# Routing of a mixture layer inside a joined attention stream: one wide comparison per sequence, sums on GpSimd, its events spread over two sequences, one bias product per sequence's logits

## What is computed

```python
def _L2_ffn_ref(x, router_w, router_bias, ...):          # x: (4, 1024, 128), 32 experts
    logits = flat @ router_w.T + router_bias
    scores = softmax(logits, axis=-1)
    topk_scores, topk_idx = top_k(scores, 4)
    topk_scores = topk_scores / clip(topk_scores.sum(-1, keepdims=True), 1e-12, None)
    ...                                                   # every token: sum over its 4 experts of score * expert(x)
```

## Time and profile before

| | |
|---|---|
| time, median of 3 runs | 2736.76 us (2734.14 to 2738.77) |
| profiled execution, its time | 2752.16 us |
| profiled execution, its span | 2750.4 us |
| PE / DVE / ACT / POOL busy | 82% / 59% / 46% / 27% |
| mean granted PE clock | 0.887 |
| the joined stream | about 660 to 2110 us of the span |

### The profile page before, as it was taken

One profiled execution on the slowest core, in us unless ns is written; L12 is line 12 of the kernel. 1 busy time (PEld: TensorE's weight loads), 2 busy tenths in 40 slices (PEclk: granted clock), 3 DMA queues, 4 the chain that ended last, 5 costly groups with the idle time before them and its releaser, 6 DMA issues. The chain is left out here.

```text
span 2750.4 us, 44402 instructions
## 1 busy us (share of the span) xinstructions
PE 2246.2 (82%) x15454; PEld 1301.6 (47%) x15454; DVE 1633.4 (59%) x3420; ACT 1260.7 (46%) x1914; POOL 752.9 (27%) x886
## 2 busy tenths in 40 slices
PE   3788878884798998999988789999997888776474
PEld 1455555562244444444444334444444775455274
DVE  6767676652674664756747787777772444554202
ACT  2334444332255666656564245565665442332143
POOL 1325253543010110200200132424221114662432
PEclk7878898987798999999999689999999999896687
DMA  2111200004020020111100011222212993110186
GB/s 64 40 48 56 48 9 2 3 1 108 28 74 29 20 61 20 38 43 38 52 28 20 19 44 56 76 61 61 64 51 88 294 314 120 42 42 17 56 275 183
DMA packets 144400, 185.07 MB, mean 67 GB/s; under 512 B 27153, under 2 KB 118450, under 8 KB 139159
## 3 DMA queue, kind: packets, MB, share of 16 engines
q1 hardware_dynamic: 103391, 136.81, 17.0%
q0 software_dynamic: 13696, 32.02, 3.7%
q10 hardware_dynamic: 27126, 13.75, 1.8%
HBM read 129.75 MB, written 52.21 MB: 66 GB/s over the span
## 5 line engine op out<-in xcount | busy, mean ns | idle before, releaser
L1766 DVE TENSOR_REDUCE a_mpart<-a_mx 128x1 f32<-128x512 f32 (+3 forms) x1216 | 744.9, 655 | 297.6 <-PE a_mx L1500 165.2
L1674 ACT ACTIVATE a_prob<-a_st 128x1024 f32<-128x1024 f32 (+3 forms) x768 | 608.1, 812 | 548.8 <-PE a_st L1533 396.4
L1497 PE MATMUL a_mx<-a_ka,a_qa 96*128 96x512 bf16 (+3 forms) x1536 | 438.1, 343 | 71.7 <-DVE a_mpart L1766 38.8
L1530 PE MATMUL a_st<-a_qa,a_ka 96*128 96x512 bf16 (+3 forms) x1536 | 422.5, 337 | 25.8 <-ACT a_prob L1674 14.5
L1548 PE MATMUL a_acc<-a_prob,a_v_aug 128*9 128x512 f32 (+3 forms) x3072 | 329.9, 507 | 0.0
L1497 PEld LDWEIGHTS a_mx<-a_ka,a_qa 96*128 96x128 bf16 x1536 | 142.8, 100 | 359.2 <-DVE a_mpart L1766 180.2
L1533 PE MATMUL a_st<-w_mask_t,identb 128*128 128x128 bf16 x1024 | 211.4, 226 | 0.0
L1530 PEld LDWEIGHTS a_st<-a_qa,a_ka 96*128 96x128 bf16 x1536 | 147.8, 100 | 127.7 <-ACT a_prob L1674 26.0
L1421 POOL DMA_INDIRECT x_rows<-l_xn,l_slots x128 | 124.9, 976 | 267.7 <-ACT a_prob L1674 256.5
L2188 PE MATMUL t_psu<-t_xsT,t_w 128*128 128x128 f32 x960 | 154.2, 296 | 25.9 <-DMA t_w<-in_l_experts 17.3
L1500 PE MATMUL a_mx<-w_mask_q,identb 128*128 128x128 bf16 x768 | 167.5, 227 | 0.0
(11 more groups left out here) (459 smaller groups left out, 4003.9 us busy)
## 6 DMA issues: line engine op xcount, KB each, us to landing
t_w<-in_l_experts SPq DMA_DIRECT2D x160, 192.0 KB, 4.3
t_w<-in_l_experts SPq DMA_DIRECT2D x40, 514.0 KB
a_qa<-q_parts_dram SPq DMA_DIRECT2D x96, 192.0 KB
a_ka<-k_parts_dram SPq DMA_DIRECT2D x96, 192.0 KB
x_rows<-zeros SPq DMA_DIRECT2D x25, 512.0 KB, 3.5
t_xs<-x_rows ACTq DMA_DIRECT2D x40, 256.0 KB, 4.8
y_rows<-t_y POOLq DMA_DIRECT2D x40, 256.0 KB
q_parts_dram<-a_parts SPq DMA_DIRECT2D x24, 256.0 KB
```

Source lines behind the costliest of these rows:

```text
L1497: ins = pe.matmul(to, qa[G % NQ][0:QK_PAD, h0 + k, qi * P:(qi + 1) * P], ka[G % NQ][:, h0 + k, lo:hi], start=not masked_first, stop=k == p ...
L1530: ins = pe.matmul(to[:, lo:HALF], ka[G % NQ][:, h, j * P:(j + 1) * P], qa[G % NQ][0:QK_PAD, h, ch * HALF + lo:(ch + 1) * HALF], start=True ...
L1674: act.activation(prob[:, k_at % NP_, 2 * pair:2 * pair + 2, lo:HALF], sring[s % 2][:, :, lo:HALF], ACT.Exp, scale=1.0 if alibi(G // NG) el ...
L1766: dve.tensor_reduce(mpart[:, G % 2, h0:h0 + per, qi, piece], slot[:, 0:per * width].rearrange("p (k w) -> p k w", k=per), X, ALU.max).then ...
```

## The change

- `r_taken`: DVE makes one comparison for all four choices (128x1024, f32) into `hits`, which lies where `hot` lies later; POOL adds the four planes in two instructions, the second into `taken` in bf16. DVE no longer waits for the result within the event; it waits for it ahead of the next sequence's comparison. `total` on PE waits for four sums rather than for sixteen.
- `r_top` is cut in two halves of four tiles, two positions apart; ranks and shares are an event of their own, `r_shares`.
- `logits`: one product of ones with the bias, repeated for the eight tiles (3x256), opens the bank; the eight tile products add to it.
- Positions, counted from the first of pass 4, a pass being 96: sequences start at 17, 35, 62 and 80; `r_exp` at +2, `r_top` at +4 and +6, `r_shares` at +8, `r_taken` at +10. `total` and `earlier` go to 97 to 107, `r_count` to 103, `r_add` to 109, `r_hot` and `r_slot` to 112 to 130, `r_tiles` to 132, `place` to 134 to 378.
- Row maxima and sums of the softmax lie in `cum` rather than in `rden`.

```diff
-        for b, pos in enumerate((18, 22, 26, 34)):
+        for b, pos in enumerate((17, 35, 62, 80)):
             put_at(at4 + pos, ("logits", b))
-            put_at(at4 + pos + 1, ("r_exp", b))
-            put_at(at4 + pos + 2, ("r_top", b))
-            put_at(at4 + pos + 3, ("r_taken", b))
+            put_at(at4 + pos + 2, ("r_exp", b))
+            for half in range(2):
+                put_at(at4 + pos + 4 + 2 * half, ("r_top", b, half))
+            put_at(at4 + pos + 8, ("r_shares", b))
+            put_at(at4 + pos + 10, ("r_taken", b))
         for half in range(2):
-            put_at(at4 + 42 + 4 * half, ("total", half))
-            put_at(at4 + 50 + 2 * half, ("earlier", half))
-        put_at(at4 + 48, ("r_count",))
-        put_at(at4 + 54, ("r_add",))
+            put_at(at4 + 97 + 4 * half, ("total", half))
+            put_at(at4 + 105 + 2 * half, ("earlier", half))
+        put_at(at4 + 103, ("r_count",))
+        put_at(at4 + 109, ("r_add",))
         for k in range(TOPK):
-            put_at(at4 + 55 + 3 * k, ("r_hot", k))
-            put_at(at4 + 57 + 3 * k, ("r_slot", k))
-        put_at(at4 + 68, ("r_tiles",))
+            put_at(at4 + 112 + 5 * k, ("r_hot", k))
+            put_at(at4 + 115 + 5 * k, ("r_slot", k))
+        put_at(at4 + 132, ("r_tiles",))
         spread([("place", b, k, t) for b in range(BATCH) for k in range(TOPK) for t in range(NT)],
-               at4 + 70, NG * STEPS * (NV - 1) + 90)
+               at4 + 134, NG * STEPS * (NV - 1) + 90)
...
+                        elif kind == "r_taken":                                   # POOL
+                            b = e[1]
+                            pool.wait_ge(hit_s, b + 1)
+                            pool.tensor_tensor(hits[:, 0:2], hits[:, 0:2], hits[:, 2:4], ALU.add).then_inc(pair_s, 1)
+                            pool.wait_ge(pair_s, b + 1)
+                            pool.tensor_tensor(taken[:, :, b * NT:(b + 1) * NT].rearrange("p e t -> p t e"), hits[:, 0], hits[:, 1], ALU.add
+                                               ).then_inc(taken_s, 1)
...
+                            pe.matmul(slot[:, 0:NE].rearrange("p (t e) -> p t e", e=E2), ones3[:],
+                                      B["l2_rbias"].unsqueeze(1).to_broadcast([PARTS, NT, E2]), start=True, stop=False)
                             for t in range(NT):
-                                to = slot[:, t * E2:(t + 1) * E2]
-                                pe.matmul(to, tile_cols(seqs[BATCH + b].xT, t), W["l2_router"][:], start=True, stop=False)
-                                ins = pe.matmul(to, ones3[:], B["l2_rbias"], start=False, stop=True)
+                                ins = pe.matmul(slot[:, t * E2:(t + 1) * E2], tile_cols(seqs[BATCH + b].xT, t), W["l2_router"][:], start=False,
+                                                stop=t == NT - 1)
...
-                            pe.wait_ge(taken_s, TOPK * BATCH)
+                            pe.wait_ge(taken_s, BATCH)
...
                         elif kind == "r_taken":                                   # DVE
                             b = e[1]
-                            if not b:
+                            if b:
+                                dve.wait_ge(taken_s, b)
+                            else:
                                 dve.wait_ge(w2_loaded, 16 * (len(second_loads) + 2))
-                            by_tile = taken[:, :, b * NT:(b + 1) * NT].rearrange("p e t -> p t e")
-                            dve.wait_ge(topped, b + 1)
-                            for k in range(TOPK):
-                                here = bcast(idx[:, k, b * NT:(b + 1) * NT], E2)
-                                if not k:
-                                    dve.tensor_tensor(by_tile, rank_b([P, NT, E2]), here, ALU.is_equal).then_inc(taken_s, 1)
-                                else:
-                                    dve.wait_ge(taken_s, TOPK * b + k)
-                                    link(dve.tensor_tensor(hit, rank_b([P, NT, E2]), here, ALU.is_equal))
-                                    dve.tensor_tensor(by_tile, by_tile, hit, ALU.add).then_inc(taken_s, 1)
-                            dve.wait_ge(taken_s, TOPK * (b + 1))
+                            dve.tensor_tensor(hits, W["rank32"][:].unsqueeze(1).unsqueeze(1).to_broadcast([P, TOPK, NT, E2]),
+                                              bcast(idx[:, :, b * NT:(b + 1) * NT], E2), ALU.is_equal).then_inc(hit_s, 1)
```

More of the change, by code:

```diff
@@ L1283, in attention_layers @@
             NE = NT * E2
-            pr, hit = (w2_flat[:, i * NE:(i + 1) * NE].rearrange("p (t e) -> p t e", e=E2) for i in range(2))
+            pr = w2_flat[:, 0:NE].rearrange("p (t e) -> p t e", e=E2)
             taken = w1[:].bitcast(BF16).rearrange("p (e t) -> p e t", t=N)
@@ L1287, in attention_layers @@
             hot = hT[:, 2:4].rearrange("p c t -> p (c t)").rearrange("p (t e) -> p t e", e=E2)
+            hits = hT[:, 2:4].rearrange("p c t -> p (c t)").rearrange("p (k t e) -> p k t e", k=TOPK, e=E2)
             eight = count[:].rearrange("p k e -> p (k e)")
@@ L1290, in attention_layers @@
                 "p (t k) -> p t k", k=8)
-            r_sum = rden[:].rearrange("p c t h -> p (c t h)")[:, 0:NT]
+            r_max, r_sum = cum[:, 0:NT], cum[:, NT:2 * NT]
             tiles, upto, adjust, ones_e = (count[:, i] for i in range(4))
@@ L1313, in attention_layers @@
             summed = sem(n + "summed")
-            r_exped, topped, taken_s, counted, hot_s, slot_s, slots_set, chosen_s, experts_in = (
-                sem(n + k) for k in ("r_exped", "topped", "taken_s", "counted", "hot_s", "slot_s", "slots_set",
+            r_exped, topped, hit_s, pair_s, taken_s, counted, hot_s, slot_s, slots_set, chosen_s, experts_in = (
+                sem(n + k) for k in ("r_exped", "topped", "hit_s", "pair_s", "taken_s", "counted", "hot_s", "slot_s", "slots_set",
                                      "chosen_s", "experts_in"))
@@ L1857, in _ @@
                             if b:
-                                dve.wait_ge(topped, b)
+                                dve.wait_ge(topped, 2 * b)
                             made_l = slot[:, 0:NE].rearrange("p (t e) -> p t e", e=E2)
-                            link(dve.tensor_reduce(r_sum, made_l, X, ALU.max))
-                            dve.tensor_tensor(pr, made_l, bcast(r_sum, E2), ALU.subtract).then_inc(ring_v, 1)
+                            link(dve.tensor_reduce(r_max, made_l, X, ALU.max))
@@ L1862, in _ @@
+                            dve.tensor_tensor(pr, made_l, bcast(r_max, E2), ALU.subtract).then_inc(ring_v, 1)
                         elif kind == "r_top":
+                            _, b, half = e
+                            if not half:
+                                dve.wait_ge(r_exped, b + 1)
+                                link(dve.tensor_reduce(r_sum, pr, X, ALU.add))
+                                link(dve.reciprocal(r_sum, r_sum))
+                                link(dve.tensor_tensor(pr, pr, bcast(r_sum, E2), ALU.mult))
@@ L1863, in _ @@
+                            for t in range(half * NT // 2, (half + 1) * NT // 2):
+                                ins = dve.max(best8[:, t], pr[:, t])
+                            link(ins)
+                            for t in range(half * NT // 2, (half + 1) * NT // 2):
+                                ins = dve.max_index(at8[:, t], best8[:, t], pr[:, t])
+                            ins.then_inc(topped, 1)
+                        elif kind == "r_shares":
                             b = e[1]
@@ L1864, in _ @@
                             mine = slice(b * NT, (b + 1) * NT)
-                            dve.wait_ge(r_exped, b + 1)
-                            link(dve.tensor_reduce(r_sum, pr, X, ALU.add))
-                            link(dve.reciprocal(r_sum, r_sum))
-                            link(dve.tensor_tensor(pr, pr, bcast(r_sum, E2), ALU.mult))
-                            for t in range(NT):
-                                ins = dve.max(best8[:, t], pr[:, t])
-                            link(ins)
@@ L1872, in _ @@
-                            for t in range(NT):
-                                ins = dve.max_index(at8[:, t], best8[:, t], pr[:, t])
-                            link(ins)
-                            dve.tensor_scalar(idx[:, :, mine].rearrange("p k t -> p t k"), at8[:, :, 0:TOPK], -1.0, float(E2), ALU.mult, ALU.add
-                                              ).then_inc(topped, 1)
+                            dve.wait_ge(topped, 2 * (b + 1))
+                            link(dve.tensor_scalar(idx[:, :, mine].rearrange("p k t -> p t k"), at8[:, :, 0:TOPK], -1.0, float(E2), ALU.mult, ALU.add))
```

## The result

The changed kernel takes 2714.8 us (median of eight runs, 2711.4 to 2726.7); the kernel before, timed beside it, 2738.9 (eight runs, 2734.1 to 2749.4). The ratio is 0.992, with a 95% interval from 0.990 to 0.994. The forecast was 2689, the range ended at 2713: faster it is, by half of what was expected, and 1.8 us outside the range.

A forecast was written before the change was run, and what follows sets the result against it. DVE was taken to bound pass 4. Passes 4 and 5, 371.2 us, would become 293.8 (two plain passes) + 14.7 (PE's work) + 8 (waits) + 7.2 (clock) = 323.7: gain 47.5, forecast 2689 us, range 2674 to 2713.

The forecast's parts named there:

- The comparison, the sums on POOL: Routing: comparison 1.21 us, saving 20.7 us of DVE over four sequences; POOL sums 1.15 and 1.3 us, nothing on the path.
- The bias product: Router logits on PE: 2.9 us per sequence instead of 3.7, so four sequences cost 11.7 us instead of 14.6.
- `r_tiles` on SP now stands beside the load of group 23, whose data are needed 36 steps later: nothing: SP's queue in pass 5: the moved store beside that load was counted as costing nothing.
- pass 5 above 165 us: Sign that the prediction is wrong, with the DVE bound moved to pass 5; forecast for that pass 150 to 160 us.
- The waits, 8 with a bound of 20: PE's waits, passes 4 and 5: 6 us for four sequences, 2 in pass 5's first group; ring covers about 2 us.
- The clock, 0.9 for each us of waiting: PE's clock in passes 4 and 5: each us of waiting brings 0.9 us of clock loss, 7.2 us in all.
- `r_hot`'s 2.86 us on POOL ... Nothing on the path: Pass 5: `r_hot` among the q, k, v pieces, which have ten steps until loaded, was counted as costing nothing.
- The scatters: 128 scatters in 244 positions instead of 308; 16 us cover before DVE's wait for `placed` in pass 6, nothing on the path.
- The spreading, which was to carry the gain: Routing in small pieces over passes 4 and 5 uses DVE's idle time, 34.7 us per pass; waits shrink but not to nothing.
- the bursts still stall PE: Rival 2, passes 4 and 5: waits 12 to 20 us, followed by low clock; gain 25 to 40, 2705 us; chance 0.14.
- Rival 3: POOL's sums lock out DVE in full: 10 us more DVE time, 19 us with the clock, 2708 us; chance 0.05.
- Rival 6: Slower: stalls spread over both passes at clock 0.83, 2747 us; decides once waits and clock loss pass 63 us; chance 0.04.

The follow-up runs named there:

- e4: The changed kernel at its new positions, with the old `r_taken` (comparisons and additions all on DVE) put back: 2732.3 us, ratio 1.000.
- e1: The changed kernel with `r_tiles` at position 133 instead of 132, behind the load of group 23: 2702.3 us, ratio 0.990; timed again, 2701.2 us, 0.988.
- e10: The kernel of e7 timed again: 2696.8 us, ratio 0.985.
- e5: The changed kernel's wide comparison, POOL sums and bias product, with all routing events at their old positions: 2702.7 us, ratio 0.990.
- e6: The changed kernel with the 32 old bias products put back, one behind each tile: 2713.9 us, ratio 0.994.
- e3: The changed kernel with `r_tiles` at 133 and pass 5's q, k, v pieces twelve positions later: 2707.6 us, ratio 0.990.
- e7: The changed kernel with `r_tiles` at 133, the softmax norm as its own event, and what follows two positions later: 2704.7 us, ratio 0.990.

## Why the prediction fell short, step by step

*The bound.* Right. DVE set the end in pass 4: with 22.0 us of its work put back, pass 4 is 20.9 us longer, and passes 4 and 5 together 17.4 (e4).

*The comparison, the sums on POOL.* Right in size: 1.24 us on average for 1.21, POOL 1.27 and 1.32 for 1.15 and 1.3. No wait for `taken` is among PE's.

*The bias product.* Too dear: 2.0 us for a sequence where 2.9 stood. The step took the distance between the two router products and the bias product of the alternating order (0.34 us a tile) as theirs alone; without the alternation a tile takes 0.22. That is 3.7 us in favour of the change (14.7 - 11.0).

*"`r_tiles` on SP now stands beside the load of group 23, whose data are needed 36 steps later: nothing".* This failed, and it cost 11.7 us (e1). It asked when the data would be needed and not what they would stand behind; the queue was named, the semaphore at its head was not. And "36 steps" counted to the group's scores, not to its maxima. It is the largest part of the missing 26 us that one edit takes away. With `r_tiles` moved the time is inside the range (2702.3 and 2701.2), and 14.4 us stay (338.1 in e1 against 323.7), from the waits and the clock below. The prediction had named pass 5 above 165 us as a sign of being wrong and DVE as what would then bound it. The sign came (168.9), and the cause was this load: without it pass 5 is 157.2.

*The waits, 8 with a bound of 20.* Mis-sized: 25.7, or 18.8 without the late load. A piece of 2.2 us was taken to be covered by the ring. It comes behind six operations of the maxima that the ring has to cover too, and then PE stands for 2.33 us. For pass 5's first group 2 us were taken; that group took 50.8 us for 43.1 before, and PE is idle 6.6 us in it where it was 2.0. PE's waits there are 3.6 us for DVE, which had 10.5 us more to do than in pass 6 before (42.34 for 31.81; the prediction said 13), and 2.7 for ACT.

*The clock, 0.9 for each us of waiting.* Mis-sized in kind. After has 25.7 us and 19.3 (0.75), e10 21.6 us (19.4 + 12.3 - 10.1) and 334.7 - 293.6 - 11.0 - 21.6 = 8.5 (0.39). There is no fixed ratio: not every wait brings the lower level.

*"`r_hot`'s 2.86 us on POOL ... Nothing on the path".* Wrong by a few us: ACT waited 10.7 us behind it, and PE for ACT 3.0 us in the rows above.

*The scatters.* Right: no DVE wait for `placed`, and pass 6 unchanged.

*The spreading, which was to carry the gain.* Wrong in weight. It was the centre of the sum, but comparison and bias product bring 28.8 us without it, and it brings 4.3 more even when its SP queue is in order (e5, e1). It is small where the bursts have been made small first. With the old `r_taken` in place the spreading would be worth some 10 us, an estimate: 371.2 before, less e4's 367.0, plus 11.7 for the late load, less 5.6 for the bias product (e6).

Of the rivals, the second comes nearest, "the bursts still stall PE": 12 to 20 us of waits, 2705. With the late load on top it is what happened. Rival 3's mechanism is in the traces, at a fraction of its price. Rival 6, the slower case, is not what was seen: the clock was 0.92 and 0.96, not 0.83, and waits plus clock loss were 45 us, below the 63 from which it decides.

Two things stay open. Whether finer pieces shorten the whole time by 4 us would take more timings; the traces show it for pass 4 alone. And nothing here divides the waits of pass 5's first group between POOL's pieces and DVE's own work, since the edit of e3 moved products of PE and work of DVE along with POOL's pieces.

## What to carry to other kernels

When an event of an order written by hand moves, look on every queue at the waits of what it is put in front of: a DMA that waits for a late result holds each load behind it, though the queue seems empty and the loads need nothing. Put such a store behind the loads of its position. Remove work from the engine that sets the pace before spreading it: in pass 4 each us of DVE work in bursts of 6.6 us cost PE nearly a us even after they were spread (e4), while with no piece above 1.3 us the clock of that pass was 0.94 to 0.98 for 0.92 and 0.93. And when a moved group of events makes one stretch shorter, look at PE's busy time beside its idle time before calling it a gain.

## What was not expected of the hardware

One 128x32 operation of DVE, 0.24 us at its next turn, took 3.11 us in after's pass 5, while POOL had three operations in a row. It ended with the last of them, and took 3.11 and 3.09 us at the same place in e4 and e6:

```profile
1692.91 1.16 POOL L1424 DMA_INDIRECT x_rows<-l_xn,l_slots  x1 [1.28 <-issue]
1693.43 3.11 DVE L1941 TENSOR_SCALAR a_count<-a_count,partition 128x32 f32<-128x32 f32 x1
...
1694.09 1.29 POOL L1447 TENSOR_TENSOR a_f<-a_f,a_hT 128x512 f32<-128x512 f32 x1
...
1695.31 1.18 POOL L1459 TENSOR_TENSOR a_parts<-a_f,a_parts 128x512 bf16<-128x512 f32 x1
...
1696.80 0.24 DVE L1941 TENSOR_SCALAR a_count<-a_count,partition 128x32 f32<-128x32 f32 x1
```

So POOL operations that follow one another without a gap can hold one DVE operation until the last has ended, not for one instruction: three times the 1.01 us of the encounter in the earlier trace rows. The other surprise is the clock. In after a wait of 1.16 us was followed by the lower level, and ones of 1.45 and 1.95 (pass 5, at 1691.0 and 1698.1) were not. In e10 waits of 1.18, 1.17, 1.19 and 1.31 us were not and ones of 1.39, 1.48, 1.71 and 2.63 were, while in e7 one of 2.62 was not. So the length of a wait alone does not tell. Twice in after, at 1564.0 and 1594.8, the level fell with no wait above 0.3 us just before; there PE had come from a sequence's small logits products.
